# Layers 1 and 3 of a four-layer board network: both units of scores masked by one VectorE instruction, and both sets of row maxima formed by one

## The reference, cut to what matters

```
q = split_heads(x @ Wq)
k = split_heads(x @ Wk)
v = split_heads(x @ Wv)
sim = jnp.einsum('bhid,bhjd->bhij', q, k) * scale
neg = -jnp.finfo(sim.dtype).max
sim = jnp.where(adjacency_mask[:, None, :, :], sim, neg)
attn = jax.nn.softmax(sim, axis=-1)
out = jnp.einsum('bhij,bhjd->bhid', attn, v)
...
h = jnp.maximum(_layernorm(x, axis=-1), 0.0)
x = x + _L1_gnn_ref(h, adj, ...)
```

## Time and profile before

| | |
|---|---|
| Median of 3 runs | 2026.94 us (2025.47 to 2035.36) |
| The profiled execution | 2030.32 us, its span 2027.9 us |
| Mean granted TensorE clock | 0.962 of full speed |
| TensorE busy | 1848.6 us, 91% |
| VectorE busy | 1404.6 us, 69% |
| ScalarE busy | 960.4 us, 47% |
| GpSimd busy | 185.8 us, 9% |

### The profile page before, as it was taken

One profiled execution on the slowest core, in us unless ns is written; L12 is line 12 of the kernel. 1 busy time (PEld: TensorE's weight loads), 2 busy tenths in 40 slices (PEclk: granted clock), 3 DMA queues, 4 the chain that ended last, 5 costly groups with the idle time before them and its releaser, 6 DMA issues.

```text
span 2027.9 us, 58099 instructions
## 1 busy us (share of the span) xinstructions
PE 1848.6 (91%) x23611; PEld 1640.9 (81%) x23611; DVE 1404.6 (69%) x3777; ACT 960.4 (47%) x3579; POOL 185.8 (9%) x297
## 2 busy tenths in 40 slices
PE   6989999989998989999999999989999999999897
PEld 5788888788887888888888887878887888888886
DVE  4767766767677767767777677676667677777674
ACT  4545445445445445445445445445445445445452
POOL 0010010110000110000110000110000100100100
PEclk9999998999999999998999999899999989989998
DMA  6000000000000000000000000000000000000000
GB/s 193 1 13 13 9 13 8 12 13 8 13 13 8 12 12 8 13 13 8 12 13 8 13 13 8 12 13 8 13 13 8 12 13 8 13 8 13 12 7 6
DMA packets 36564, 30.62 MB, mean 15 GB/s; under 512 B 11600, under 2 KB 36176, under 8 KB 36368
## 3 DMA queue, kind: packets, MB, share of 16 engines
q1 hardware_dynamic: 36368, 27.48, 4.5%
HBM read 19.08 MB, written 8.39 MB: 14 GB/s over the span
## 4 chain that ended last, share of the span: by engine, by line
PE 72%; DVE 18%; issue 5%; ACT 4%; POOL 1%; DMA 0%; DVEq 0%; SPq 0%; POOLq 0%
PE ps L484 65%; PE ps L596 3%; PE ps L670 3%; DVE small L1070 3%; DVE xn L1082 3%; ACT probs L900 2%; DVE f L1229 1%; DVE small L1076 1%; DVE f L1227 1%; DVE x L1234 1%; DVE oT L969 1%; DVE kT L1129 1%; DVE x L1169 1%; DVE probs L1159 1%; PE ps L793 1%
## 5 line engine op out<-in xcount | busy, mean ns | idle before, releaser
L484 PE MATMUL ps<-hT,w_hi 128*128 128x256 f32 x2560 | 489.9, 285 | 5.0 <-DVE w_lo L969 3.2
L484 PE MATMUL ps<-w_hi,hT 128*128 128x256 f32 (+1 forms) x1536 | 424.4, 344 | 0.0
L484 PEld LDWEIGHTS ps<-hT,w_hi 128*128 128x128 f32 x2560 | 409.0, 191 | 8.7 <-DVE w_lo L969 3.6
L900 ACT ACTIVATE probs<-probs,small 128x64 f32<-128x64 f32 x1024 | 341.9, 337 | 108.2 <-DVE small L1149 106.5
L484 PE MATMUL ps<-hT,w_lo 128*128 128x256 f32 x1280 | 334.0, 283 | 0.0
L464 POOL TENSOR_TENSOR small<-small,consts 128x1 f32<-128x1 f32 x256 | 150.8, 589 | 1804.0 <-DVE small L1078 1804.0
L484 PEld LDWEIGHTS ps<-w_hi,hT 128*128 128x128 f32 x1536 | 268.1, 188 | 42.7 <-DVE wh L1201 11.5
L484 PE MATMUL ps<-w_hi,oT 128*128 128x256 f32 x768 | 212.1, 340 | 53.8 <-DVE oT L969 44.6
L484 PE MATMUL ps<-w_lo,hT 128*128 128x256 f32 (+1 forms) x768 | 250.0, 337 | 0.0
L484 PEld LDWEIGHTS ps<-hT,w_lo 128*128 128x128 f32 x1280 | 244.8, 191 | 0.0
L484 PEld LDWEIGHTS ps<-w_hi,oT 128*128 128x128 f32 x768 | 153.1, 220 | 72.8 <-DVE oT L969 61.9
(11 more groups left out here) (126 smaller groups left out, 3399.2 us busy)
## 6 DMA issues: line engine op xcount, KB each, us to landing
x_next<-x SPq DMA_DIRECT2D x32, 256.0 KB, 2.6
out<-x SPq DMA_DIRECT2D x32, 256.0 KB, 2.2
raw_lo<-mats SPq DMA_DIRECT2D x6, 1024.0 KB, 9.9
adj<-adjq SPq DMA_DIRECT2D x64, 16.0 KB, 1.9
raw_hi<-mats SPq DMA_DIRECT2D x1, 1024.0 KB, 11.5
adjT<-adjt SPq DMA_DIRECT2D x64, 8.0 KB, 2.3
raw_lo<-mats SPq DMA_DIRECT2D x1, 512.0 KB, 8.3
raw_consts<-board_consts SPq DMA_DIRECT2D x1, 451.5 KB, 3.0
```

The costliest lines, as they stand in the source:

```text
L484: return nc.tensor.matmul(o, lhsT, rhs, start=start, stop=stop, skip_group_check=True)
L900: last = fn(p, p, ACT.Exp, bias=ROWMAX[s][:, row:row + 1], accum_out=ROWSUM[s][:, row:row + 1])
```

## The change

For layers 1 and 3 (`a > 0`) VectorE does nothing at the `mask` and `max` steps of the first unit (`cj == 0`). At the second unit's `mask` step it waits for the scores of both, masks both in one instruction of 512 elements a row, and raises `masked` by 2. At the second unit's `max` step one reduction forms all 8 maxima and raises `rowmax` by 2. Layer 0, the table of turns, and the lists of all other engines are as they were.

```
+                elif k in ("mask", "max") and a > 0:
+
+                    u, m, j, cj = i
+                    if cj == 0:
+                        return
+                    p = PR[s][:, j, :].rearrange("p (c b k) -> p c b k", c=2, k=SQ)
+                    if k == "mask":
+                        dve.wait_ge(sm["s_ps"], v.eight[u])
+                        mask = rows(MASKA[s][:, :]).unsqueeze(1).broadcast_to([P, 2, NB, SQ])
+                        both = PS[:, 4 * s + m - 1:4 * s + m + 1, 0:TOK].rearrange("p c (b k) -> p c b k", k=SQ)
+                        stt(p, both, scale, mask, ALU.mult, ALU.add).then_inc(sm["masked"], 2)
+                    else:
+                        dve.wait_ge(sm["masked"], v.eight[u])
+                        nc.vector.reduce_max(ROWMAX[s][:, (m - 1) * NB:(m + 1) * NB],
+                                             PR[s][:, j, :].rearrange("p (b k) -> p b k", k=SQ), AX_X, negate=True
+                                             ).then_inc(sm["rowmax"], 2)
                 elif k == "mask":
```

## The result

The changed kernel is slower: 2064.45 us (median of 4 runs, 2058.87 to 2069.61) against 2031.15 us (4 runs, the three shown before and one more). The ratio is 1.016, with a 95% interval from 1.011 to 1.0209. Measured a second time it was 2060.47 us (6 runs) against 2036.19 us (11 runs), ratio 1.0129 [1.0097, 1.0162]. So the change costs 24 to 33 us. The forecast was 26.3 us and 2053 us, with a range from 2040 to 2063, so the time lies just above it.

What follows compares the result with a forecast made beforehand. TensorE, 91% busy, was taken to bind, waiting in P and Q on a VectorE-ScalarE relay. 15 x 1.13 + 16 x 0.52 + 2 x 0.5 = 26.3 us gave 2053 us on the shown runs' median, range 2040 to 2063.

Steps and rivals of the forecast that it cites:

- Size of the new instructions: 512-wide mask and reduction on VectorE: 0.68 us each, taken from a 512-wide addition, with bounds 0.68 and 0.83.
- slip by 0.3 to 0.53: In P, slot 0's late normalisation delays TensorE's transposes and slot 1's scores; 0.41 us taken, moving slot 1's mask.
- Block P: Loop stretch with slot 0's layer 1 softmax, then slot 1's layer 3: TensorE's dense stretch starts 1.13 us later, 15 times.
- Block Q: Loop stretch with slot 1's layer 1 softmax, then slot 0's layer 3: exponentials and what follows 0.52 us later, 16 times.
- so all P are alike: The 16 VectorE waits for scores before a mask, 21.7 us together, were taken as 1.36 us each, 15 in P.
- What P or Q loses is hardly given back there: Outside the blocks TensorE runs nearly without a gap, 45.43 of 46.77 us from P's end to Q's start.
- single sets: Slot 0's set alone in the first turn and slot 1's last set: 2 x 0.5 us, at most 0.53 each.
- Rival 2: No change: TensorE's 1.3 us idle behind P hides the delay; about 2027 us, at most 10 from it; chance 0.08.
- rival 4: Merging saves nothing: instructions of 0.83 us, about +0.55 a block, 17 us more, 2070 us; chance 0.04.
- 1: Faster: VectorE's saved time is worth its full price, 64 x 0.27 = 17 us come back, 2010 us; chance 0.04.
- 3: Only the plain delay: both blocks lose 0.53, 31 x 0.53 = 16 us, 2043 us; chance 0.14.
- P's 13.65: From P's layer 1 mask to the oT wait that ends it: 12.52 us was to become 13.65.

Runs made afterwards that it cites:

- The delay alone: Kernel before with VectorE unchanged, but in layers 1 and 3 ScalarE waits for both units' maxima before the first unit's exponentials: 2074.31 us, ratio 1.0203.
- Layer 1 alone: Merged mask and maxima in layer 1 only, layer 3 as in the kernel before: 2044.96 us, ratio 1.0059 against the kernel before.
- Layer 3 alone: Merged mask and maxima in layer 3 only, layer 1 as in the kernel before: 2050.68 us, ratio 1.0102 against the kernel before.

## Why the prediction was right or wrong

- *What bounds it, and the direction*: right. VectorE's saved time had no value, and the start of the exponentials had its full price. The delay alone (no merging) lost 41 us, and the changed kernel took up 22 us of added VectorE work with no block longer at full clock. The Trainium skill's "Perfetto Trace Analysis" (Optimizing Scalar/DVE Operations) had the case: grouping pays on a saturated engine, and breaking up may pay on one that only delays others. The runs agree, with VectorE at 69%. The rule in the Trainium skill's "VectorE: DVE Perf Modes" (Rules for kernel authors) to minimize the number of operations would have given the wrong sign: 128 fewer cost 24 to 33 us.
- *Size of the new instructions*: 0.68 forecast, 0.683 measured.
- *"The dependent reduction starts some 0.03 behind the mask's end, as now"*: wrong, it is 0.11. The exponentials moved by 0.60, not by 0.53, and a set with its reduction right behind saved 0.18 us of VectorE and not 0.27. A 256-wide row was taken for a 512-wide instruction. The 512-wide sum of layer 2 shows the 0.11.
- *"TensorE's transposes, and slot 1's scores behind them, slip by 0.3 to 0.53. I take 0.41"*: mis-sized. Slot 1's mask in P slipped by 0.67. Layer 1 alone gives 0.54 of it, the upper end of my bounds and not the middle. Layer 3 alone gives 0.14, a wait that wasn't in the sum: the double mask needs the second unit's scores (0.06) and starts late as a wide instruction (0.08).
- *Block P*, at full clock: 1.13 forecast, 1.39 at TensorE's last wait, 1.37 up to Q's first mask (6.36 + 54.30 against 5.69 + 53.60). *Block Q*: 0.52 forecast, 0.68 at TensorE's wait, and about 0.6 up to the next P (5.34 and 55.29 against 4.90 and 55.10, one stretch at full clock of the changed kernel). 15 x 0.24 + 16 x 0.1 = 5 us were missing in the sum, 31 instead of 26, if every stretch ran at full clock.
- *"... so all P are alike"*: wrong, and over all turns this made the term of P too high and not too low. They are alike up to the second set. Behind it, 8 of 15 turns of the kernel before (11 in its second trace) had a lower granted clock, and there TensorE's own matmuls had already put the last oT product at 13.1 to 13.9 instead of 12.52. Over all turns a P cost 0.88 and 0.70 at that product, not 1.39, and less than the 1.13 forecast.
- *"What P or Q loses is hardly given back there"*: right for the stretch behind P. From the last oT product to Q's first mask it took 47.96 and 48.12 us in the mean before, and 48.08 and 47.85 after. Mask to mask, with the stretch behind it, a P really cost 0.72 and a Q 0.78, together with the single sets 24 us between the first and the last set. Rival 2 looked for the time in the stretch behind P, and what was hidden was hidden inside P.
- *"It was 3.4 above the median of the runs shown ... and by that I forecast 2053 us"*: the step rests on the median of three, 2026.94, and that was low: four runs gave 2031.15, and 16, 13 and 11 more runs 2032.42, 2033.73 and 2036.19. As a difference, 26.3 us lies between the two measurements (24 and 33).
- *The time outside the range*: 2064.45 is 11.2 above the forecast. 4.2 of it is the baseline. The stretch ahead of the first set of layer 1, for which the sum had no term, was 6.6 longer in the profiled execution and 7.0 in the second pair of traces. Of the terms that the sum did have, the slip and the late reduction were up to 5 too small, and the turns of lower clock took some 7 off (24 instead of 31), so that 26.3 agrees with the measured 24 to 33 in part by luck. The upper end itself was set loosely: half the way from 2053 to rival 4's 2070 is 2061.5, not 2063.
- *The rivals*: 1 and 2 are ruled out as they stand by the intervals. 3 (both blocks lose only 0.53) is ruled out by P's 1.39. It was right that the place behind the oT piece costs little, 0.13. What it left out is the delay of the second set on top of the slip of the first. 4 (merging saves nothing) by the 0.683.
- *The profile forecast*: VectorE's busy time fell by 14.4 us, not by 17. A set with its reduction right behind was busy for 1.50 of its 1.57 us, with two gaps of 0.03 to 0.04, and is now busy for 1.28 of 1.39, with one of 0.11: 0.22 us less, 14 us over 64 sets. P's 13.65 became 13.91. ScalarE's idle time in front of a layer 1 set's exponentials went from 1.33 to 1.93 us, +0.60 for a forecast of about 0.5. "TensorE's busy time stays" was wrong: it grew from 1848.6 to 1868.5 us, some 8 of this in the windows of the start (44.15 against 52.07), where the granted clock was lower.

## What to carry to other kernels

Two instructions in a row are often a pipeline with the next engine. Before merging them, ask who starts on the first one's result, and price the merge as (time to the pair's result) minus (time to the first's result), once for each place where that engine is the one that ends last. The saving counts only where VectorE itself has no wait up to the next thing TensorE needs. And a forecast in absolute time stands on the kernel before's median: with three runs that spread by 10 us, its error (4 us) was about as large as that of the sum (5 us).

## What was not expected of the hardware

- A VectorE instruction of 512 elements a row that waits for one before it starts 0.11 us behind that one's end, one of 256 elements 0.03 to 0.04 behind, in the mask and reduction here and in the sum of layer 2. The count to which the waiting semaphore is compared doesn't matter.
- The first 61 to 69 us of the same instructions ran with a granted TensorE clock of 0.97 or 0.85, and about 7 us longer at the lower. Later on, no stretch between the two sets of a block ever had less than 1.00, in any trace: the lowered clock fell behind the second set, into P's second half and the dense stretches. From P's second set to Q these were 53.59 to 57.33 us long in the first trace of the kernel before, with 1.00 to 0.91 granted.
- From the first to the last layer set the changed kernel took 1979.90 and 1976.74 us, the kernel before 1952.84 and 1956.56. That is 24 us, less than the 31 of the full-clock stretches. The mean granted clock between P's second set and Q does not tell them apart (0.952 and 0.942 before, 0.951 and 0.963 after). What does is where it was lower: in P's second half TensorE was slow before the change in 8 and 11 turns, and the delay then cost it less.
